# Attention operands laid out by dimension, four heads to a load

## The chip, the cores and the metric

The kernel runs on one core of one Trainium2 chip. The metric is the device time of one execution in microseconds (us), the median of several runs; lower is better.

## The reference

The model is a stack of six residual blocks on x of shape (2, 2048, 256) in float32: an expert layer, attention with 16 heads and a position bias, the expert layer again, a second expert layer, differential attention, and the second expert layer again. The change touches the two attentions. In short:

```python
# first attention, 16 heads of 16
q, k, v = x @ Wq.T + bq, x @ Wk.T + bk, x @ Wv.T + bv
scores = einsum('bhqd,bhkd->bhqk', q, k) / sqrt(16) + slope[h] * (pos_k - pos_q)
y = softmax(causal(scores)) @ v
# second attention, two maps of 16 heads of 16, values of 32
a1, a2 = softmax(causal(q1 @ k1.T * scale)), softmax(causal(q2 @ k2.T * scale))
y = layernorm((a1 - lam[h] * a2) @ v) * (1 - lambda_init) @ Wc
```

## The kernel before

The kernel runs phase after phase. The names in the profile begin with the phase: `ba` is the first attention, `ea` the second, `bp` and `ep` the projections ahead of them, `bo` and `eo` the output products behind them; `ae`, `ce`, `de`, `fe` are the experts.

**Levels.** Queries and keys are float32, but PE multiplies bfloat16. So `project_phase` splits each into three bfloat16 levels (a value is the sum of its levels) and stores them in DRAM, in `lv`, one tensor each for queries and keys, in `ea` for each map: a row of 2048 positions (4 KB) for each level, head and dimension. A score is the sum of six products of levels: the key levels 0, 1, 2 with query level 2 - n, and so on. `KP` = 96 rows of contraction hold them: query level 0 beside key levels 0, 1, 2 (48 rows), query level 1 beside key levels 0, 1 (32 rows), query level 2 beside key level 0 (16 rows), after the order in which the `lq[3 - n]` of the loader names them. On the query side a level is copied n times, on the key side n levels are read. Ahead of these 96 stand `F` rows: in `ba` 12, nine for the position bias and three (`BIAS_MAX`) for the maxima; in `ea` three for the maxima alone.

**Steps.** `attention_phase` works in steps of `HV` = 4 heads (in `ea` two heads of two maps): 8 steps in `ba`, 16 in `ea`. In a step, PE computes all scores twice. The *maxima* products (L1504 into `psA`) have a query to a row; VectorE (DVE) takes the maximum of each row (L1642), splits it in three levels, PE transposes them, and GpSimd's queue (POOL) writes them as three rows into `qx` (`store_maxima`, L1476), where ones in `kx` meet them. The *scores* (L1529 into `psB`) then come out with the maximum subtracted, ScalarE (ACT) exponentiates them (L1624), and PE multiplies them with the values `vx` (L1544). `step_order` writes out the order in which PE, DVE and ACT take the pieces. From slot `NEXT_AT` = 19 of 40 units on, the maxima of the *next* step are mixed in, so PE waits there (L1587) for the next step's `qx` and `kx`; both have two buffers.

**The loader.** SyncE (SP) issues all of this in order, per step (`body`, L1444): the row sums of the step before out to DRAM and back in another shape (`sums_out`); a wait that PE has done with the other buffer; `load` of group 0 (two heads, or the first map) and of `vx`; `inverses_in` (the inverted sums to DRAM, a wait, and four broadcast loads into `rec`); `load` of group 1; and the results to `yT` when POOL has scaled them (L1481). A group has 14 loads: for n = 3, 2, 1 and each of two heads one of queries and one of keys, and two of constants. The core of it:

```python
sp.dma_start(qx[at:at + n * DH, s, hh, :],
             lq[3 - n, rows, :].unsqueeze(0).broadcast_to((n, DH, S)))
sp.dma_start(kx[at:at + n * DH, s, hh, :], lk[0:n, rows, :])
```

Of the kernel before, what the change touches and what calls it, by code (L numbers as in the profile page):

```python
# [1299 lines left out]

def attention_phase(nc, name, D, C, lvq, lvk, vd, yT, sums, sgn, maps, qc, kc, F, MR, s_m, st0):
    two = maps == 2
    steps = B * NHEAD * maps // HV
    KB = F + KP
    shared = qc.shape[0] == F
    VCOL = vd.shape[-1] // KT
    YR = P // maps
    nld = 14
    SR = DH if maps == 1 else VW - 1
    SC = HV * S // P  # L1310
    with Scope(nc, name) as sc:
# [13 lines left out]

        s_ld = [[sc.sem(f"ld{s}{g}") for g in range(2)] for s in range(2)]
        s_v = [sc.sem(f"v{s}") for s in range(2)]
# [64 lines left out]
        with nc.Block() as block:  # L1392

            @block.sync
            def _(sp):
                def load(st, s, *groups):
                    for g in groups:
                        if two:
                            lq, lk, r0, own = lvq[g], lvk[g], st * (2 * DH), slice(g, HV, 2)
                        else:  # L1400
                            lq, lk, r0, own = lvq[0], lvk[0], st * (HV * DH) + g * 2 * DH, slice(2 * g, 2 * g + 2)
                        at = F
                        for n in (3, 2, 1):
                            for h, hh in enumerate(range(HV)[own]):
                                rows = ds(r0 + h * DH, DH)
                                sp.dma_start(qx[at:at + n * DH, s, hh, :],
                                             lq[3 - n, rows, :].unsqueeze(0).broadcast_to((n, DH, S))).then_inc(s_ld[s][g], 16)
                                sp.dma_start(kx[at:at + n * DH, s, hh, :], lk[0:n, rows, :]).then_inc(s_ld[s][g], 16)
                            at += n * DH
                        for dst, src in ((qx, qc), (kx, kc)):  # L1410
                            sp.dma_start(dst[0:F, s, own, :],
                                         src.unsqueeze(1).broadcast_to((F, 2, S)) if shared else
                                         src[ds((st * HV + 2 * g) * F, 2 * F), :].rearrange("(h f) s -> f h s", h=2)
                                         ).then_inc(s_ld[s][g], 16)
                    if 0 in groups:
                        sp.dma_start(vx[:, s].rearrange("p k c -> p (k c)"),
                                     vd[ds(st, 1)].rearrange("g p c -> p (g c)")).then_inc(s_v[s], 16)

# [25 lines left out]
                def body(st, s, use, prev, nxt, before):  # L1444
                    if prev:
                        sums_out(st - 1, 1 - s, use + s - 1)
                    if nxt:
                        if prev:
                            sp.wait_ge(s_av, st * NU)
                        load(st + 1, 1 - s, 0)  # L1450
                    if prev:
                        inverses_in(st - 1, 1 - s, use + s - 1)
                    if nxt:
                        load(st + 1, 1 - s, 1)
                    if prev:
                        for Q in range(QB):
                            result_out(st - 1, 1 - s, Q)

                load(0, 0, 0, 1)

# [36 lines left out]
            def _(pe):  # L1497
                def maxima(i, s, slot):
                    t, k0, m, heads = ITEMS[i]
                    runs = [(hh, b * BLK, k0, m) for b, hh in enumerate(heads)] if len(heads) == 2 else \  # L1500
                        [(heads[0], 0, k0, BLK), (heads[0], BLK, k0 + BLK, m - BLK)]
                    for hh, at, k, n in runs:
                        diag = k + n == (t + 1) * P
                        last = nc.tensor.matmul(psA[:, slot, at:at + n], qx[0:KB, s, hh, t * P:(t + 1) * P],  # L1504
                                                kx[0:KB, s, hh, k:k + n], start=True, stop=not diag)
                        if diag:
                            last = nc.tensor.matmul(psA[:, slot, at + n - P:at + n], C["identb"], C["maskA"],  # L1507
                                                    start=False, stop=True)
                    last.then_inc(s_af, 1)
# [43 lines left out]

                for g in range(2):
                    pe.wait_ge(s_ld[0][g], 16 * nld)
                n = 0
# [15 lines left out]
                def body(st, s, use, prev, nxt, before):  # L1572
# [5 lines left out]
                    for k, a in order:  # L1578
                        if k in RING_KINDS:
                            slot = slots[(k, a)][0]  # L1580
                            pe.wait_ge(*freed[(k, a)])
                        if k == "A":
                            d, i = a
                            if d and not arrived:
                                arrived = True
                                for g in range(2):
                                    pe.wait_ge(s_ld[1 - s][g], 16 * nld * (use + s + 1))  # L1587
                            maxima(i, 1 - s if d else s, slot)
                        elif k == "M":
                            levels(*a, st, s, slot)  # L1590
                        elif k == "C":
                            difference(a, st, s, slot)
                        elif k == "B":
                            scores(*a, st, s, not prev)
                        elif k == "V" and a < 0:
                            values(NU - 1, st - 1, 1 - s)
                        elif k == "V":
                            values(a, st, s)
# [287 lines left out]
def bf16(a):  # L1886
    return np.asarray(a, np.float32).astype(mybir.dt.np(BF16))
# [12 lines left out]

BIAS_ROWS, BIAS_MAX = 12, 3

# [7 lines left out]
def constants():  # L1910
# [28 lines left out]
    for st in range(steps):  # L1939
        for hh in range(HV):  # L1940
            for l, s in enumerate(three_levels(np.float32(SLOPES[st % (NHEAD // HV) * HV + hh]))):
                r = 3 * l if l == 0 else 3 * l + 3
                q[st, hh, r], k[st, hh, r] = -(j // BLK) * BLK, s
                q[st, hh, r + 1], k[st, hh, r + 1] = s, j // P * P
                q[st, hh, r + 2], k[st, hh, r + 2] = s, j % P
            k[st, hh, BIAS_MAX:BIAS_MAX + 3] = 1
    return {
        "c_f32": np.concatenate([f[n] for n, _ in F32_CONSTS], 1).astype(np.float32),
        "c_f16": row(p).astype(np.float16), "c_bf16": bf16(np.concatenate([h[n] for n, _ in BF16_CONSTS], 1)),
        "c_q": bf16(q.reshape(-1, S)), "c_k": bf16(k.reshape(-1, S)),  # L1950
        "c_q1": bf16(np.zeros((3, S))), "c_k1": bf16(np.ones((3, S))),
    }
# [33 lines left out]
def macaron_kernel(nc, D, out):  # L1986
# [6 lines left out]
    routed = scratch("routed", (T + P, H))  # L1993
    lv = [scratch(f"lv{i}", (3, B * H, S), BF16) for i in range(4)]
    vd0, vd1 = scratch("vd0", (B * NHEAD // 4, P, KT * 4 * VW)), scratch("vd1", (B * NHEAD // 2, P, KT * 2 * VW))
    yT, sums = scratch("yT", (B * NHEAD * VW, S)), scratch("sums", (2, 2, HV * S))
    with Scope(nc, "all") as sc:
# [27 lines left out]
        with Scope(nc, "b") as f:  # L2025
            xnT = f.sb("xnT", [P, HC, T])
            norm_phase(nc, "bn", x, xnT, C["ident"])
            project_phase(nc, "bp", D, xnT, [(D["L0_wq"], D["L0_bqk"], DH ** -0.5), (D["L0_wk"], None, 1.0)],
                          D["L0_wv"], D["L0_bv"], lv[0:2], vd0, False)
        attention_phase(nc, "ba", D, C, lv[0:1], lv[1:2], vd0, yT, sums, None, 1, D["c_q"], D["c_k"], BIAS_ROWS, BIAS_MAX, s_m, 0)  # L2030
        output_phase(nc, "bo", D, C, x, yT, D["L0_wo"], 1.0, False)
        experts0("c", 1)
        experts1("d", 0)
        with Scope(nc, "e") as g:
            sgn = g.sb("sgn", [P, B * NHEAD // 2])
            lambda_phase(nc, "el", D, C, sgn[:])
            with Scope(nc, "ef") as f:
                xnT = f.sb("xnT", [P, HC, T])
                norm_phase(nc, "en", x, xnT, C["ident"])
                s = DH ** -0.5  # L2040
                project_phase(nc, "ep", D, xnT, [(D["L1_wq1"], None, s), (D["L1_wk1"], None, 1.0),
                                                 (D["L1_wq2"], None, s), (D["L1_wk2"], None, 1.0)],
                              D["L1_wv"], None, lv, vd1, True)
            attention_phase(nc, "ea", D, C, [lv[0], lv[2]], [lv[1], lv[3]], vd1, yT, sums, sgn, 2, D["c_q1"], D["c_k1"], 3, 0, s_m,
                            B * NHEAD // HV)
# [12 lines left out]
def lay_out(I):  # L2058
# [7 lines left out]
    D["L0_w"] = np.concatenate(up + [I["L0_ffn_w2"].transpose(0, 2, 1)], 2)  # L2066
    for n in "qkv":
        D["L0_w" + n] = by_chunk(I["L0_attn_W" + n].T)
    D["L0_bqk"] = np.concatenate([I["L0_attn_b" + n].reshape(HC, P).T for n in "qk"], 1)
    D["L0_bv"] = I["L0_attn_bv"]  # L2070
# [7 lines left out]
    for k, n in (("rg", "routed_gate_w"), ("ru", "routed_up_w"), ("rd", "routed_down_w")):  # L2078
        D["L1_" + k] = I["L1_ffn_" + n]
    for n in ("q1", "q2", "k1", "k2", "v", "c"):  # L2080
        D["L1_w" + n] = by_chunk(I["L1_attn_W" + n])
# [19 lines left out]
```

## Time and profile before

| | us |
|---|---|
| median of 3 runs | 6779.74 (6776.26 to 6789.61) |
| the profiled execution | 6790.24 |
| its span, first to last instruction | 6788.4 |
| `ba`, first load issued to last score | about 904 to 2022 |
| `ea`, the same | about 3756 to 5944 |
| mean granted clock of PE | 0.877 |

The two attention phases make up nearly half of the span. Rows of the profile name an engine, the line of the kernel, and what is written from what (`ba_kx<-lv`); "<-" behind a wait names what ended it. SPq is SP's queue of transfers, PE the matmul engine. A DMA share is the mean over the core's 16 DMA engines, so 0.13 can mean two of them busy all the time.

### The profile page before, as it was taken

Reading aid. Unit: us, or ns where it says so; the run is one execution under the profiler, and the core shown is the slowest. Engines: PE = TensorE matmul, PEld = TensorE weight load, DVE = VectorE, ACT = ScalarE, POOL = GpSimd, SP = SyncE. Lnnn points to the kernel's source line nnn. Section 1 sums busy time; section 2 is a strip of 40 time slices with the busy share of each in tenths; the row PEclk is TensorE's granted clock in tenths of the full one; section 3 lists DMA queues with packets and bytes.
Section 4 is the critical chain, followed back from the end, with each engine's and each line's share of the span. In section 5 each row is a group of like instructions: output and inputs, shape, how many; then the busy total and the mean of one; then the engine's idle time right before and its main releaser. Section 6 shows DMA issues by size and latency. Waiting matters only on the chain. (4 is left out here: it accounts for less than half of the span.)

```text
span 6788.4 us, 95548 instructions
## 1 busy us (share of the span) xinstructions
PE 5217.8 (77%) x30112; PEld 2794.8 (41%) x30112; DVE 3361.2 (50%) x5679; ACT 2483.8 (37%) x4942; POOL 1576.2 (23%) x1276
## 2 busy tenths in 40 slices
PE   6466448888787466489968688878888888976997
PEld 3355223333235355247953233323333333343696
DVE  7511646666544821311148566756666666533111
ACT  2011106555561011122211266656655655612221
POOL 2388300000101178433324000000000000002332
PEclk9688769999898678789989699989998999988998
DMA  2376431112203177507955211111111111011498
GB/s 93 98 150 138 132 111 41 42 42 59 64 21 116 31 169 149 137 2 243 330 174 163 64 34 35 55 43 35 40 53 41 34 43 53 15 63 35 146 325 272
DMA packets 454298, 660.17 MB, mean 97 GB/s; under 512 B 97984, under 2 KB 308992, under 8 KB 448672
## 3 DMA queue, kind: packets, MB, share of 16 engines
q1 hardware_dynamic: 383232, 544.50, 25.6%
q0 software_dynamic: 70656, 110.44, 8.0%
q8 instruction: 228, 3.74, 0.2%
q14 instruction: 182, 1.49, 0.1%
HBM read 489.33 MB, written 164.20 MB: 96 GB/s over the span
## 5 line engine op out<-in xcount | busy, mean ns | idle before, releaser
L1642 DVE TENSOR_REDUCE ea_mx<-ea_psA 128x1 f32<-128x1024 f32 (+7 forms) x1280 | 1317.6, 1061 | 697.5 <-PE ea_psA L1507 491.4
L1624 ACT ACTIVATE ea_pr<-ea_psB 128x512 f32<-128x512 f32 (+3 forms) x2560 | 1229.7, 535 | 934.6 <-PE ea_psB L1529 514.5
L1504 PE MATMUL ea_psA<-ea_kx,ea_qx 99*128 99x512 bf16 (+3 forms) x2560 | 730.0, 363 | 285.4 <-DMA ea_kx<-in_c_k 256.0
L1642 DVE TENSOR_REDUCE ba_mx<-ba_psA 128x1 f32<-128x1024 f32 (+7 forms) x640 | 657.4, 1061 | 381.5 <-PE ba_psA L1507 282.5
L1529 PE MATMUL ea_psB<-ea_qx,ea_kx 99*128 99x512 bf16 (+3 forms) x2560 | 782.7, 354 | 29.0 <-issue 21.0
L1624 ACT ACTIVATE ba_pr<-ba_psB 128x512 f32<-128x512 f32 (+3 forms) x1280 | 610.7, 535 | 494.8 <-PE ba_psB L1529 260.3
L1544 PE MATMUL ea_psO<-ea_pr,ea_vx 128*32 128x512 f32 (+3 forms) x5120 | 612.2, 551 | 1.9 <-ACT ea_pr L1624 0.4
L1504 PE MATMUL ba_psA<-ba_kx,ba_qx 108*128 108x512 bf16 (+3 forms) x1280 | 371.7, 369 | 198.2 <-DMA ba_kx<-in_c_k 181.3
L1504 PEld LDWEIGHTS ea_psA<-ea_kx,ea_qx 99*128 99x128 bf16 x2560 | 217.9, 100 | 695.1 <-issue 383.4
L1476 POOL DMA_DIRECT2D ea_qx<-ea_mT x192 | 106.0, 559 | 1546.3 <-DVE ea_mT L1664 1521.9
L1529 PEld LDWEIGHTS ea_psB<-ea_qx,ea_kx 99*128 99x128 bf16 x2560 | 242.3, 99 | 501.0 <-ACT ea_pr L1624 315.2
L1529 PE MATMUL ba_psB<-ba_qx,ba_kx 108*128 108x512 bf16 (+3 forms) x1280 | 387.3, 354 | 12.9 <-issue 6.4
L1544 PE MATMUL ba_psO<-ba_pr,ba_vx 128*32 128x512 f32 (+3 forms) x2560 | 305.1, 549 | 1.2 <-ACT ba_pr L1624 0.4
L1504 PEld LDWEIGHTS ba_psA<-ba_kx,ba_qx 108*128 108x128 bf16 x1280 | 109.2, 101 | 409.0 <-issue 231.9
L1476 POOL DMA_DIRECT2D ba_qx<-ba_mT x96 | 53.1, 560 | 804.2 <-DVE ba_mT L1664 804.0
L1507 PE MATMUL ea_psA<-all_cb 128*128 128x128 bf16 x1024 | 229.4, 235 | 0.0
L690 POOL DMA_INDIRECT acc<-ce_y,c_idx x128 | 205.1, 1602 | 46.0 <-issue 35.2
L1529 PEld LDWEIGHTS ba_psB<-ba_qx,ba_kx 108*128 108x128 bf16 x1280 | 120.1, 99 | 231.6 <-ACT ba_pr L1624 154.7
L690 POOL DMA_INDIRECT acc<-ae_y,a_idx x128 | 204.7, 1599 | 46.2 <-issue 36.1
L1532 PE MATMUL ea_psB<-all_cb 128*128 128x128 bf16 x1024 | 209.2, 222 | 0.0
L1481 POOL TENSOR_TENSOR ea_rec<-ea_osb,ea_rec 128x2048 f32<-128x2048 f32 x16 | 72.5, 4532 | 541.1 <-DMA ea_rec<-sums 541.1
L767 DVE TENSOR_TENSOR ae_h<-ae_sg,ae_psH 128x256 f32<-128x256 f32 x64 | 27.0, 422 | 303.0 <-ACT ae_sg L748 269.0
(522 smaller groups left out, 8297.0 us busy)
## 6 DMA issues: line engine op xcount, KB each, us to landing
de_wg<-in_L_rg SPq DMA_DIRECT2D x64, 512.0 KB
de_wu<-in_L_ru SPq DMA_DIRECT2D x64, 512.0 KB
de_wd<-in_L_rd SPq DMA_DIRECT2D x64, 512.0 KB
fe_wg<-in_L_rg SPq DMA_DIRECT2D x64, 512.0 KB
fe_wu<-in_L_ru SPq DMA_DIRECT2D x64, 512.0 KB
fe_wd<-in_L_rd SPq DMA_DIRECT2D x64, 512.0 KB
ae_w<-in_L_w SPq DMA_DIRECT2D x64, 384.0 KB, 3.7
ce_w<-in_L_w SPq DMA_DIRECT2D x64, 384.0 KB
```

The costliest lines, as they stand in the source:

```text
L690: nc.gpsimd.indirect_dma_start(out=acc[a], out_offset=column(n, a), in_=y[:, n % RING, a, :], in_offset=None, bounds_check=bound, oob_is_e ...
L767: nc.vector.tensor_tensor(h[:, u % 2, :], sg[:, u % 2, :], psH[:, u % 2, 1, :], ALU.mult).then_inc(s_hh, 1)
L1476: pool.dma_start(qx[MR:MR + 3, s, hh, t0 * P:(t0 + tc) * P].rearrange("l (t q) -> l t q", q=P), mT[hh * 3 * tc:(hh + 1) * 3 * tc, k, :]).t ...
L1481: nc.gpsimd.tensor_tensor(rec[:, s, :], osb[:, s, :], rec[:, s, :], ALU.mult).then_inc(s_z, 1)
L1504: last = nc.tensor.matmul(psA[:, slot, at:at + n], qx[0:KB, s, hh, t * P:(t + 1) * P], kx[0:KB, s, hh, k:k + n], start=True, stop=not diag)
L1507: last = nc.tensor.matmul(psA[:, slot, at + n - P:at + n], C["identb"], C["maskA"], start=False, stop=True)
L1529: last = nc.tensor.matmul(psB[:, slot, off:BLK], kx[0:KB, s, hh, kt * P:(kt + 1) * P], qx[0:KB, s, hh, Q * BLK + off:(Q + 1) * BLK], start ...
L1532: last = nc.tensor.matmul(psB[:, slot, off:off + P], C["identb"], C["maskB"], start=False, stop=True)
L1544: last = nc.tensor.matmul(psO[hh * VW:(hh + 1) * VW, off:BLK], vx[:, s, kt, vcol:vcol + VW], pr[:, j % 2, hh, off:BLK], start=(kt == 0), s ...
L1624: nc.scalar.activation(pr[:, j % 2, hh, off:BLK], psB[:, exp_slot(n, s), off:BLK], ACT.Exp).then_inc(s_exp, 1)
L1642: v.tensor_reduce(out, src, AX.X, ALU.max).then_inc(s_ar, 1)
```

## The change

The levels are stored in DRAM by dimension, with the four heads of a step side by side, so that the rows of one dimension of four heads are 16 KB in a piece. To that end the columns of the projection weights are reordered on the way in (`together`), and in `ea` the stores of the two maps interleave (`of_map`). `load` is split into `load_queries` (three loads of queries for all four heads, one of the bias rows in `ba`, and `vx`) and `load_keys` (three, and one in `ba`); queries go where group 0 went, keys where group 1 went. The rows of levels now begin at row 0, the nine bias rows follow, and the three rows of the maxima stand last; the ones in `kx` that meet them are loaded once, for both buffers, at the start of a phase. The maxima products leave out these last three rows (`KA`); the scores have them (`KB`). Of the 28 operand loads of a step and that of `vx`, 9 are left in `ba` and 7 in `ea`.

```diff
--- before.py
+++ after.py
@@ -1298,14 +1298,14 @@
-def attention_phase(nc, name, D, C, lvq, lvk, vd, yT, sums, sgn, maps, qc, kc, F, MR, s_m, st0):
+def attention_phase(nc, name, D, C, lvq, lvk, vd, yT, sums, sgn, maps, qc, kc, ones, F, s_m, st0):
     two = maps == 2
     steps = B * NHEAD * maps // HV
-    KB = F + KP
-    shared = qc.shape[0] == F
+    KA, KB = KP + F, KP + F + 3
+    MR = KA
     VCOL = vd.shape[-1] // KT
     YR = P // maps
-    nld = 14
+    nld = 8 if F else 6
     SR = DH if maps == 1 else VW - 1
@@ -1323,7 +1323,7 @@
-        s_ld = [[sc.sem(f"ld{s}{g}") for g in range(2)] for s in range(2)]
+        s_ld, s_one = [sc.sem(f"ld{s}") for s in range(2)], sc.sem("one")
         s_v = [sc.sem(f"v{s}") for s in range(2)]
@@ -1393,28 +1393,27 @@
             def _(sp):
-                def load(st, s, *groups):
-                    for g in groups:
-                        if two:
-                            lq, lk, r0, own = lvq[g], lvk[g], st * (2 * DH), slice(g, HV, 2)
-                        else:
-                            lq, lk, r0, own = lvq[0], lvk[0], st * (HV * DH) + g * 2 * DH, slice(2 * g, 2 * g + 2)
-                        at = F
-                        for n in (3, 2, 1):
-                            for h, hh in enumerate(range(HV)[own]):
-                                rows = ds(r0 + h * DH, DH)
-                                sp.dma_start(qx[at:at + n * DH, s, hh, :],
-                                             lq[3 - n, rows, :].unsqueeze(0).broadcast_to((n, DH, S))).then_inc(s_ld[s][g], 16)
-                                sp.dma_start(kx[at:at + n * DH, s, hh, :], lk[0:n, rows, :]).then_inc(s_ld[s][g], 16)
-                            at += n * DH
-                        for dst, src in ((qx, qc), (kx, kc)):
-                            sp.dma_start(dst[0:F, s, own, :],
-                                         src.unsqueeze(1).broadcast_to((F, 2, S)) if shared else
-                                         src[ds((st * HV + 2 * g) * F, 2 * F), :].rearrange("(h f) s -> f h s", h=2)
-                                         ).then_inc(s_ld[s][g], 16)
-                    if 0 in groups:
-                        sp.dma_start(vx[:, s].rearrange("p k c -> p (k c)"),
-                                     vd[ds(st, 1)].rearrange("g p c -> p (g c)")).then_inc(s_v[s], 16)
+                def load_queries(st, s):
+                    at = 0
+                    for n in (3, 2, 1):
+                        src = lvq[3 - n, ds(st * HV * DH, HV * DH), :].rearrange("(d h) s -> d (h s)", h=HV)
+                        sp.dma_start(qx[at:at + n * DH, s].rearrange("p h s -> p (h s)"),
+                                     src.unsqueeze(0).broadcast_to((n, DH, HV * S))).then_inc(s_ld[s], 16)
+                        at += n * DH
+                    if F:
+                        sp.dma_start(qx[KP:KA, s].rearrange("p h s -> p (h s)"), qc[ds(st * F, F), :]).then_inc(s_ld[s], 16)
+                    sp.dma_start(vx[:, s].rearrange("p k c -> p (k c)"),
+                                 vd[ds(st, 1)].rearrange("g p c -> p (g c)")).then_inc(s_v[s], 16)
+
+                def load_keys(st, s):
+                    at = 0
+                    for n in (3, 2, 1):
+                        sp.dma_start(kx[at:at + n * DH, s].rearrange("p h s -> p (h s)"),
+                                     lvk[0:n, ds(st * HV * DH, HV * DH), :].rearrange("l (d h) s -> l d (h s)", h=HV)
+                                     ).then_inc(s_ld[s], 16)
+                        at += n * DH
+                    if F:
+                        sp.dma_start(kx[KP:KA, s].rearrange("p h s -> p (h s)"), kc[ds(st * F, F), :]).then_inc(s_ld[s], 16)
@@ -1447,16 +1446,19 @@
                             sp.wait_ge(s_av, st * NU)
-                        load(st + 1, 1 - s, 0)
+                        load_queries(st + 1, 1 - s)
                     if prev:
...
                     if nxt:
-                        load(st + 1, 1 - s, 1)
+                        load_keys(st + 1, 1 - s)
                     if prev:
...
-                load(0, 0, 0, 1)
+                load_queries(0, 0)
+                load_keys(0, 0)
+                for u in range(2):
+                    sp.dma_start(kx[KA:KB, u], ones.unsqueeze(1).broadcast_to((3, HV, S))).then_inc(s_one, 16)
@@ -1501,8 +1503,8 @@
                         diag = k + n == (t + 1) * P
-                        last = nc.tensor.matmul(psA[:, slot, at:at + n], qx[0:KB, s, hh, t * P:(t + 1) * P],
-                                                kx[0:KB, s, hh, k:k + n], start=True, stop=not diag)
+                        last = nc.tensor.matmul(psA[:, slot, at:at + n], qx[0:KA, s, hh, t * P:(t + 1) * P],
+                                                kx[0:KA, s, hh, k:k + n], start=True, stop=not diag)
                         if diag:
@@ -1551,8 +1553,8 @@
-                for g in range(2):
-                    pe.wait_ge(s_ld[0][g], 16 * nld)
+                pe.wait_ge(s_ld[0], 16 * nld)
+                pe.wait_ge(s_one, 32)
                 n = 0
@@ -1583,8 +1585,7 @@
                                 arrived = True
-                                for g in range(2):
-                                    pe.wait_ge(s_ld[1 - s][g], 16 * nld * (use + s + 1))
+                                pe.wait_ge(s_ld[1 - s], 16 * nld * (use + s + 1))
                             maxima(i, 1 - s if d else s, slot)
@@ -1898,7 +1899,7 @@
-BIAS_ROWS, BIAS_MAX = 12, 3
+BIAS_ROWS = 9
@@ -1939,16 +1940,15 @@
             for l, s in enumerate(three_levels(np.float32(SLOPES[st % (NHEAD // HV) * HV + hh]))):
-                r = 3 * l if l == 0 else 3 * l + 3
+                r = 3 * l
                 q[st, hh, r], k[st, hh, r] = -(j // BLK) * BLK, s
...
                 q[st, hh, r + 2], k[st, hh, r + 2] = s, j % P
-            k[st, hh, BIAS_MAX:BIAS_MAX + 3] = 1
     return {
...
         "c_f16": row(p).astype(np.float16), "c_bf16": bf16(np.concatenate([h[n] for n, _ in BF16_CONSTS], 1)),
-        "c_q": bf16(q.reshape(-1, S)), "c_k": bf16(k.reshape(-1, S)),
-        "c_q1": bf16(np.zeros((3, S))), "c_k1": bf16(np.ones((3, S))),
+        "c_q": bf16(q.transpose(0, 2, 1, 3).reshape(-1, HV * S)),
+        "c_k": bf16(k.transpose(0, 2, 1, 3).reshape(-1, HV * S)), "c_one": bf16(np.ones((3, S))),
     }
@@ -1991,7 +1991,7 @@
     routed = scratch("routed", (T + P, H))
-    lv = [scratch(f"lv{i}", (3, B * H, S), BF16) for i in range(4)]
+    lvq, lvk = (scratch(n, (3, B * NHEAD * 2 * DH, S), BF16) for n in ("lvq", "lvk"))
     vd0, vd1 = scratch("vd0", (B * NHEAD // 4, P, KT * 4 * VW)), scratch("vd1", (B * NHEAD // 2, P, KT * 2 * VW))
@@ -2026,8 +2026,8 @@
             project_phase(nc, "bp", D, xnT, [(D["L0_wq"], D["L0_bqk"], DH ** -0.5), (D["L0_wk"], None, 1.0)],
-                          D["L0_wv"], D["L0_bv"], lv[0:2], vd0, False)
-        attention_phase(nc, "ba", D, C, lv[0:1], lv[1:2], vd0, yT, sums, None, 1, D["c_q"], D["c_k"], BIAS_ROWS, BIAS_MAX, s_m, 0)
+                          D["L0_wv"], D["L0_bv"], [lvq[:, 0:B * H], lvk[:, 0:B * H]], vd0, False)
+        attention_phase(nc, "ba", D, C, lvq, lvk, vd0, yT, sums, None, 1, D["c_q"], D["c_k"], D["c_one"], BIAS_ROWS, s_m, 0)
         output_phase(nc, "bo", D, C, x, yT, D["L0_wo"], 1.0, False)
@@ -2038,10 +2038,11 @@
                 s = DH ** -0.5
+                of_map = lambda a, g: a.rearrange("l (r g) s -> l g r s", g=2)[:, g]
                 project_phase(nc, "ep", D, xnT, [(D["L1_wq1"], None, s), (D["L1_wk1"], None, 1.0),
                                                  (D["L1_wq2"], None, s), (D["L1_wk2"], None, 1.0)],
-                              D["L1_wv"], None, lv, vd1, True)
-            attention_phase(nc, "ea", D, C, [lv[0], lv[2]], [lv[1], lv[3]], vd1, yT, sums, sgn, 2, D["c_q1"], D["c_k1"], 3, 0, s_m,
+                              D["L1_wv"], None, [of_map(a, g) for g in range(2) for a in (lvq, lvk)], vd1, True)
+            attention_phase(nc, "ea", D, C, lvq, lvk, vd1, yT, sums, sgn, 2, None, None, D["c_one"], 0, s_m,
                             B * NHEAD // HV)
@@ -2064,9 +2065,11 @@
     D["L0_w"] = np.concatenate(up + [I["L0_ffn_w2"].transpose(0, 2, 1)], 2)
-    for n in "qkv":
-        D["L0_w" + n] = by_chunk(I["L0_attn_W" + n].T)
-    D["L0_bqk"] = np.concatenate([I["L0_attn_b" + n].reshape(HC, P).T for n in "qk"], 1)
+    together = lambda a, heads: a.reshape(-1, NHEAD // heads, heads, DH).transpose(0, 1, 3, 2).reshape(-1, H)
+    for n in "qk":
+        D["L0_w" + n] = by_chunk(together(I["L0_attn_W" + n].T, HV))
+    D["L0_wv"] = by_chunk(I["L0_attn_Wv"].T)
+    D["L0_bqk"] = np.concatenate([together(I["L0_attn_b" + n], HV).reshape(HC, P).T for n in "qk"], 1)
     D["L0_bv"] = I["L0_attn_bv"]
@@ -2077,7 +2080,9 @@
         D["L1_" + k] = I["L1_ffn_" + n]
-    for n in ("q1", "q2", "k1", "k2", "v", "c"):
+    for n in ("q1", "q2", "k1", "k2"):
+        D["L1_w" + n] = by_chunk(together(I["L1_attn_W" + n], HV // 2))
+    for n in ("v", "c"):
         D["L1_w" + n] = by_chunk(I["L1_attn_W" + n])
```

## Rows read from the trace of the kernel before

**Rows 1.** the page, its first line and part 1 (busy us, share, xinstructions)
```profile
span 6788.4 us, 95548 instructions
...
PE 5217.8 (77%) x30112; PEld 2794.8 (41%) x30112; DVE 3361.2 (50%) x5679; ACT 2483.8 (37%) x4942; POOL 1576.2 (23%) x1276
```

**Rows 2.** waits of PE (total us, times, longest): `ba`, `ea`, and the whole span
```profile
PE ba_psA L1504 <- DMA ba_kx<-in_c_k: 122.5, 6, 21.6
...
PE ea_psA L1504 <- DMA ea_kx<-in_c_k: 202.3, 14, 15.3
PE ea_psA L1504 <- DVE ea_mx L1642: 24.9, 43, 0.7
...
PE ea_psA L1504 <- DMA ea_kx<-in_c_k: 256.0, 15, 53.6
...
PE ba_psA L1504 <- DMA ba_kx<-in_c_k: 181.3, 7, 58.8
```

**Rows 3.** timeline of PE at one step's stall (start, length, what, [idle before])
```profile
1189.28 0.26 PE L1504 MATMUL ba_psA<-ba_kx,ba_qx 108*128 108x128 bf16 x1 [19.98 <-DMA ba_kx<-in_c_k]
```

**Rows 4.** timeline of SP's queue, one `ba` step (start us, length us)
```profile
1125.28 0.83 SPq L1406 DMA_DIRECT2D ba_qx<-lv  x1
...
1138.50 0.36 SPq L1416 DMA_DIRECT2D ba_vx<-vd  x1
1138.93 0.41 SPq L1428 DMA_DIRECT2D sums<-ba_sm  x1
1157.51 1.73 SPq L1433 DMA_DIRECT2D ba_rec<-sums  x4
1159.43 0.78 SPq L1406 DMA_DIRECT2D ba_qx<-lv  x1
...
1166.95 2.60 SPq L1408 DMA_DIRECT2D ba_kx<-lv  x1
...
1174.15 0.32 SPq L1411 DMA_DIRECT2D ba_kx<-in_c_k  x1
1175.01 0.44 SPq L1442 DMA_DIRECT2D yT<-ba_rec  x1
```

**Rows 5.** windows; the last three numbers are PE clock, DMA share, GB/s
```profile
1137.00:1145.50 8.50, 8.50 (x60) 3.20 (x59) 6.95 (x7) 6.09 (x12) 0.00 (x0) 1.00 0.87 176
...
1158.90:1163.70 4.80, 4.80 (x30) 1.48 (x30) 3.59 (x4) 3.81 (x8) 0.00 (x0) 1.00 0.90 200
1163.70:1167.00 3.30, 3.30 (x21) 1.20 (x20) 2.70 (x3) 2.41 (x6) 2.45 (x1) 1.00 0.18 58
1167.00:1172.50 5.50, 2.30 (x15) 0.47 (x12) 2.89 (x7) 2.54 (x5) 2.09 (x1) 1.00 0.19 75
...
1182.00:1186.00 4.00, 0.00 (x0) 0.00 (x0) 0.00 (x0) 0.00 (x0) 0.00 (x0) 0.50 0.13 51
...
3981.00:3984.50 3.50, 3.50 (x25) 0.94 (x25) 2.71 (x4) 2.98 (x7) 0.00 (x0) 1.00 0.21 81
```

**Rows 6.** DMA issues: count, KB each, median us to landing
```profile
ea_qx<-lv SPq DMA_DIRECT2D x64, 192.0 KB
...
ba_vx<-vd SPq DMA_DIRECT2D x8, 1024.0 KB, 18.9
ba_rec<-sums SPq DMA_DIRECT2D x32, 256.0 KB, 4.5
...
ba_qx<-in_c_q SPq DMA_DIRECT2D x16, 96.0 KB
...
ea_qx<-in_c_q SPq DMA_DIRECT2D x32, 24.0 KB
```

**Rows 7.** PE by form: busy us, mean ns, for both contraction lengths of L1504
```profile
L1504 PE MATMUL ba_psA<-ba_kx,ba_qx 108*128 108x512 bf16 x896 | 300.6, 399 | 15.1 <-DVE ba_mx L1642 13.3
...
L1504 PE MATMUL ea_psA<-ea_kx,ea_qx 99*128 99x512 bf16 x1792 | 590.0, 392 | 27.6 <-DVE ea_mx L1642 24.4
```

**Rows 8.** the page, part 3: DMA queue, packets, MB, share of 16 engines
```profile
q8 instruction: 228, 3.74, 0.2%
```

## The prediction

> **What bounds the kernel now.** I read the page first: TensorE (PE) has the largest share, 77%, but this is a mean over many stages [rows 1]. Next I asked what PE waits for in the two attention phases. There one wait stands out: the first maxima product of a step (L1504, behind the waits for `s_ld`) waits for the operand loads of the next step. It is 122.5 us in six steps of the first phase (`ba`) and 202.3 us in fourteen of the second (`ea`). The next wait of PE there is 24.9 us in all of `ea`, and the longest single waits, 58.8 and 53.6 us, are the first loads of each phase [rows 2]. In the timeline one such wait is 19.98 us of nothing, ended by the last load [rows 3]. So in these twenty steps the loads set the period, one for one; time taken off them is gained until the wait is gone.
>
> Then I followed SP's queue through one `ba` step [rows 4]. Loads of the first two heads go out from 1125.28, `vx` at 1138.50, and the write of the inverses at 1138.93; SP then waits for that write until 1157.51, issues `rec`, the loads of the other two heads from 1159.43 to 1174.5, then yT. PE goes on at 1189.28. The chain is 1189.28 − 1125.28 = 64.0 us. Is it issue or transfer? The windows tell [rows 5]: from 1182 to 1186 the DMA share is 0.13 and 51 GB/s move. 0.13 × 16 = 2.1, so two engines work and fourteen are idle, at 51 / 2 = 25.5 GB/s each. From 1167 to 1172.5 it is 0.19 × 16 = 3.0 engines. These are the loads of two and three copies. SP issues a load in under 0.8 us, but some stretch, to 2.6 us here [rows 4], where it waits for room: the engines are behind, not SP.
>
> I add up the fullest engine, in KB of 1024 bytes, with the sizes of [rows 6]. A load of three copies, 192 KB over three engines, gives it 64; of two copies, 128 KB over two, 64; of one, 64 KB over 16, 4. Half a step's loads (four of each) are 528, the constants 16 (two loads of 8 per engine), `vx` 64, `rec` (four loads of 256 KB) 64. So the first half has 528 + 16 + 64 = 608 KB or 24.4 us at 25.5 GB/s, the second with `rec` 608 KB or 24.4 us. That is 49 of the 64 us. The other 15 us are the start of each half and the stretches in which all sixteen engines move `vx`, `rec`, yT and the loads of one copy: 176 to 200 GB/s at a share of 0.87 to 0.90, or 13 to 14 GB/s for each engine, half of 25.5 [rows 5].
>
> **The change, part by part.** *Fewer loads.* Queries go as three loads (three, two, one copies) of four heads, keys likewise, so 28 operand loads become 8 or 6. The leading dimension of each is still the number of copies, so I expect three, two and sixteen engines again. Per engine the three-copy load carries 768 / 3 = 256 KB, the two-copy 512 / 2 = 256, the one-copy 16: 528 KB, as now. `ba`'s constants are 9 rows of 16 KB, 16 KB on each of nine engines, as now. So for `ba`: **no byte less on the fullest engine**, and the work that SP saves (some 10 issues of 0.7 to 0.8 us in each half) is hidden behind it: SP would only wait sooner, at the inverses and at the end. If that cover were gone, the issues would cost about 14 us a step. The rule "Use all 16 engines" in the Trainium skill (DMA: Bandwidth & Descriptors, Rules for kernel authors) says this of such loads: a leading dimension of c copies confines a transfer to at most c engines; the trace agrees, with 0.13 and 0.19 of sixteen. That rule speaks against a large gain here, as the rows do.
>
> *No constants in `ea`.* 16 KB less on the fullest engine in each half: 32 KB, 32.8 / 25.5 = 1.3 us a step, 14 × 1.3 = 18 us.
>
> *Longer rows.* One row is now 16 KB, not 4. No row of the loads prices this. One end is no gain. The other is the best rate of a three-engine stretch, 81 / 3 = 27 GB/s [rows 5]: 557 kB in 20.6 us, not 21.8, so 1.2 us a half. Most stretches lie at 25.5, so I take 0.5 us, 1.0 a step: 6 us in `ba`, 14 us in `ea`. A far row is the instruction queue: 228 packets of 16.4 KB took 0.2% (0.15 to 0.25) of sixteen engines' span, 0.7 to 1.2 us each, or 14 to 23 GB/s [rows 8]. Another destination, so I leave it out of the sum; at 17 GB/s each half would grow by 11 us, 440 us in all.
>
> *Order.* Queries and `vx` stay ahead of the inverses, keys behind `rec`, where the halves were. SP now reaches the inverses earlier, but the write waits behind the same queries on the same engines. yT may go out about 5 us sooner and then runs beside the three-copy keys in place of the two-copy ones: the same loss, moved.
>
> *First loads.* PE's first wait now has `vx` ahead of the keys and two loads of ones behind them: 64 + 32 KB more in `ba`, 98 kB, 3.9 us, less 1 us for rows; in `ea` 32 + 32 − 32 (no constants) = 32 KB, 1.3 us, less 1. Together +3 us.
>
> *Rows of maxima.* They move behind the others; the maxima product now reads 105 or 96 rows, not 108 or 99. A product of 512 columns takes 399 ns with 108 rows and 392 with 99 [rows 7]: nothing. POOL's stores keep number and size. They may stand behind one 16 KB packet, 0.6 us at 25.5 GB/s; PE asks for them units of work later. Uncovered, it would be 0.5 us three times a step. The stores of the projection keep runs of 1 KB, every second row in `ea`: nothing.
>
> **Sum**: −6 − 14 − 18 + 3 = −35 us. The profiled execution, 6790 us with its 6788.4 us span, would become 6755. It stands 10.5 us above the median shown, 6779.74, so against that I say **6745 us**, 0.5% faster. In `ba` the wait of 20.4 us stays above 18, in `ea` 14.5 becomes 12.
>
> **The rivals.** *A, the number of loads sets the time.* If each load carried a cost of its own, 20 fewer would undo the stall: 6780 − 325 [rows 2] = 6455 us. Against it: the two engines that are never idle. The Trainium skill (same page and section) advises coalescing many small transfers, since under 64 KB mostly overhead is paid; by that advice the one-copy loads at least would be cheaper, but no run here shows it. Chance 0.05.
>
> *B, nothing that can be measured*, which for this kernel is anything within 0.2% (14 us). Long rows bring nothing, and the 18 us of the constants are eaten by `vx` in the first wait or by a collision that moves: 6766 to 6793, about 6772. Chance 0.17.
>
> *C, slower: the slow start of a broadcast lasts as long as the broadcast.* From 1163.7 to 1167, the first 3.3 us of three-copy loads, the engines move 58 GB/s at a share of 0.18; later, at 0.19, it is 75 [rows 5]. Three engines begin on copies of the same rows in step, and something they share holds them up; after one load of 64 KB each they are out of step. Now the first broadcast is four times as long. At 58 GB/s, 786 kB take 13.6 us, at 78 10.1: 3.5 us, of which 0.8 are paid today, so +2.7 us a step, 20 × 2.7 = 54. With the −35 it is +19: **6799 us**. From 1.8 us a step upwards it turns the sign; if the keys, which aren't broadcast, suffered too, 6853. For it: the slow starts recur. Against it: it may be the start of a queue, not the copying. Chance 0.16, the 16 KB packet of [rows 8] included.
>
> **How the numbers follow.** The forecast (gains of 14 to 90 us) has 0.62, A 0.05, B 0.17, C 0.16. Faster by over 0.2%: 0.62 + 0.05 = 0.67; within: 0.17; slower: 0.16. The low end: 6745 less 32 us if the slow starts vanish (0.8 × 2 × 20) and less 28 for the rest of the row bound (0.7 × 2 × 20), rounded: 6685. The high end takes in B and C's 6799 with the rows bringing nothing (+10 to 20): 6815. Outside lie A, the dear end of C and the slow packet.
>
> **What would show it.** Right: PE's waits on the loads near 116 us in `ba` and 170 in `ea`; again stretches at 0.13 and 51 GB/s, before the inverses land and before PE goes on; SP's queue with four or five short issues and no stretched ones; a gap from the first query load to `rec` still near 31 us. A is right if the gaps are gone; C if the stretch near 58 GB/s grows from 3 to 10 us or more. The forecast is wrong if the two-engine stretches are absent, or if the engine rate with 16 KB rows isn't 25 to 27 GB/s.

## The result, and the profile after

The changed kernel takes **7007.6 us** (median of 4 runs, 7006.5 to 7012.4) against 6782.7 for the one before: a ratio of 1.0333, 95% interval 1.0315 to 1.0351. It is 225 us slower, where 35 us less was forecast.

The page of the changed kernel, first line and part 1. The span has grown by 216 us. PE is busy only 25 us longer than in [rows 1], with the same products at a mean granted clock of 0.868 for 0.877, so nearly all of the time went into waiting.

```profile
span 7004.6 us, 94559 instructions
...
PE 5242.8 (75%) x30108; PEld 2791.8 (40%) x30112; DVE 3370.2 (48%) x5679; ACT 2483.8 (35%) x4942; POOL 1570.4 (22%) x1276
```

Waits of PE in the changed kernel, in `ba` and then in `ea` (total us, times, longest):

```profile
PE ba_psA L1506 <- DMA ba_kx<-in_c_k: 177.0, 6, 31.0
PE ba_psA L1506 <- DMA ba_kx<-in_c_one: 69.3, 1, 69.3
...
PE ea_psA L1506 <- DMA ea_kx<-lvk: 249.0, 14, 19.4
PE ea_psA L1553 <- POOL ea_rec L1483: 93.4, 15, 18.5
PE ea_psA L1506 <- DMA ea_kx<-in_c_one: 63.3, 1, 63.3
```

Against [rows 2] the loads cost 54.5 us more in `ba` and 46.7 in `ea`, and the two first waits 20.2 more. In `ea` PE also waits for POOL's product with the inverses (L1553). 18.5 us of it stand at the end of the phase, as they did before; the other 74.9 us, in fourteen steps, are new. POOL's product needs `rec`, which now lands later, so I read this as the same lateness seen earlier in the step. Together these are 196 of the 216 us.

SP's queue in one `ba` step of the changed kernel (start us, length us):

```profile
1135.53 2.37 SPq L1400 DMA_DIRECT2D ba_qx<-lvq  x3
1138.12 0.28 SPq L1404 DMA_DIRECT2D ba_qx<-in_c_q  x1
1138.59 0.36 SPq L1405 DMA_DIRECT2D ba_vx<-vd  x1
1146.78 0.35 SPq L1427 DMA_DIRECT2D sums<-ba_sm  x1
1172.87 1.72 SPq L1432 DMA_DIRECT2D ba_rec<-sums  x4
1174.69 2.00 SPq L1411 DMA_DIRECT2D ba_kx<-lvk  x3
1176.78 0.34 SPq L1416 DMA_DIRECT2D ba_kx<-in_c_k  x1
```

The issues are few and short, as the change says: the queries and `vx` are out in 3.4 us, the keys in 2.4. But from the first query load to `rec` it is 37.3 us, not 32.2 [rows 4], and from `rec` until PE goes on at 1210.54 it is 37.7, not 31.8: each half has grown by 5 to 6 us. The windows of this step show where (the last two numbers are DMA share and GB/s):

```profile
1149.00:1158.50 9.50, 9.50 (x75) 4.08 (x71) 6.69 (x8) 5.90 (x14) 0.00 (x0) 1.00 0.19 57
...
1190.50:1199.00 8.50, 0.00 (x0) 0.00 (x0) 0.00 (x0) 0.00 (x0) 0.00 (x0) 0.50 0.18 54
```

A share of 0.18 to 0.19 is three busy engines, as from 1167 to 1172.5 before [rows 5]. But they move 54 to 57 GB/s and not 75, for some 9 us in each half, with the queries (copies) and with the keys (three levels) alike.

### The profile page after: what moved, and what is told of

The parts are those of the page before. It is cut to its first block and busy times, and to the rows that moved or that the text cites. A ratio compares the mean times of both kernels' runs of the same rounds, so it can differ in the third digit from the quotient of the medians.

```text
span 7004.6 us, 94559 instructions
## 1 busy us (share of the span) xinstructions
PE 5242.8 (75%) x30108; PEld 2791.8 (40%) x30112; DVE 3370.2 (48%) x5679; ACT 2483.8 (35%) x4942; POOL 1570.4 (22%) x1276
## 5 line engine op out<-in xcount | busy, mean ns | idle before, releaser
L1506 PE MATMUL ea_psA<-ea_kx,ea_qx 96*128 96x512 bf16 (+3 forms) x2560 | 734.9, 364 | 341.5 <-DMA ea_kx<-lvk 249.0
L1506 PE MATMUL ba_psA<-ba_kx,ba_qx 105*128 105x512 bf16 (+3 forms) x1280 | 370.1, 367 | 264.1 <-DMA ba_kx<-in_c_k 177.0
L1506 PEld LDWEIGHTS ea_psA<-ea_kx,ea_qx 96*128 96x128 bf16 x2560 | 218.8, 100 | 753.1 <-issue 309.1
L1506 PEld LDWEIGHTS ba_psA<-ba_kx,ba_qx 105*128 105x128 bf16 x1280 | 109.0, 101 | 473.6 <-issue 206.5
L1546 PEld LDWEIGHTS ea_psO<-ea_pr,ea_vx 128*32 128x32 f32 x5120 | 102.0, 109 | 176.8 <-ACT ea_pr L1625 88.5
```

The source lines that it names most:

```text
L1506: last = nc.tensor.matmul(psA[:, slot, at:at + n], qx[0:KA, s, hh, t * P:(t + 1) * P], kx[0:KA, s, hh, k:k + n], start=True, stop=not diag)
L1546: last = nc.tensor.matmul(psO[hh * VW:(hh + 1) * VW, off:BLK], vx[:, s, kt, vcol:vcol + VW], pr[:, j % 2, hh, off:BLK], start=(kt == 0), s ...
```

## The experiments

Two theories stood first. *P, place*: engines that write SBUF partitions 32 apart at the same time share a way in and halve each other. With three copies as the leading dimension, engine 0 should have rows 0 to 15 and engine 2 rows 32 to 47, and both go through them in step. (No row here names the engine of a row; this division is assumed, and the loads below fit it.) *S, source*: they read the same rows, or levels at a fixed distance, in step. A third, *O*, was the order: all queries, `vx` and one-copy loads early.

### The loads alone

This kernel leaves the model out and makes test loads, one after the other, each waited for but the last four. It ran once, so each time in the table is a single measurement. In `far` the groups come from far-apart rows, in `copies` they are the same rows; the second number is the first partition written.

```python
far = lambda l, n, w=HV * S: src.rearrange("(l r) s -> l r s", l=l)[:, 0:n, 0:w]
copies = lambda l, n, w=HV * S: src[0:n, 0:w].unsqueeze(0).broadcast_to((l, n, w))
tests = (("two4", 0, far(2, 4)), ("two8", 0, far(2, 8)), ("two16", 0, far(2, 16)), ("two32", 0, far(2, 32)),
         ("two32at32", 32, far(2, 32)), ("two32copies", 0, copies(2, 32)), ("three16", 0, far(3, 16)),
         ("three16at32", 32, far(3, 16)), ("wide48", 0, far(3, 16).rearrange("l r s -> r l s")))
```

> This kernel leaves the whole model out: it loads x and the constants, makes eleven test loads one after another, each waited for, and writes x out. The loads carry rows of 16 KB with two or three groups of rows as the leading dimension, so that two or three engines share the work. A row alone took 0.61 us in the changed kernel, so two16 (16 rows per engine) is about 9.8 us plus some 2.5 us of latency. Theory P (the place in SBUF: engines that write partitions 32 apart at the same time halve each other): two4, two8 and two16 undisturbed, 5, 7.5 and 12.5 us; two32 (partitions 0 to 31 and 32 to 63) doubled, about 42 us and not 22; two32copies the same 42; three16 about 20 and not 12.5; two32at32 and three16at32 show whether the halves 0 to 63 and 64 to 127 are separate (22 and 12.5) or not (42 and 20). Theory S (the source in DRAM: copies of one row, or levels at a fixed distance, are read in step): two32copies and two32 differ, and three16at32 is like three16. Short rows: short16 (4 KB rows) 5 us, a few tenths more with a collision; fourshort about 12.5 us. wide48 (dimension first, 16 engines) 4 to 6.5 us.

In SP's queue the next start is the end of a test. The trace drops the digits that end a name: `m_two` at 32.29 is two16, at 44.81 two32, and `m_three` is three16. `m_short` and `m_fourshort` are three groups of 16 rows of 4 KB at partition 0, one load and four.

```profile
32.29 13.06 SPq L2023 DMA_DIRECT2D m_two<-in_c_q  x2
...
44.81 0.54 SPq L2023 DMA_DIRECT2D m_two<-in_c_q  x1
79.13 0.64 SPq L2023 DMA_DIRECT2D m_two32at<-in_c_q  x1
101.36 0.53 SPq L2023 DMA_DIRECT2D m_two32copies<-in_c_q  x1
138.69 0.76 SPq L2023 DMA_DIRECT2D m_three<-in_c_q  x1
157.44 0.72 SPq L2023 DMA_DIRECT2D m_three16at<-in_c_q  x1
169.90 0.63 SPq L2023 DMA_DIRECT2D m_wide<-in_c_q  x1
177.58 0.73 SPq L2025 DMA_DIRECT2D m_short<-in_c_q  x1
183.88 2.94 SPq L2028 DMA_DIRECT2D m_fourshort<-in_c_q  x4
197.91 0.40 SPq L1982 DMA_DIRECT2D out_x<-all_x  x1
```

| load, two or three groups of 16 KB rows | partitions | us |
|---|---|---|
| two16, 16 apart | 0 to 31 | 12.5 |
| two32, 32 apart | 0 to 63 | 34.3 |
| two32copies, the same source rows | 0 to 63 | 37.3 |
| two32at32, 32 apart across 64 | 32 to 95 | 22.2 |
| three16 | 0 to 47 | 18.8 |
| three16at32 | 32 to 79 | 12.5 |
| wide48, 16 engines, 48 rows | 0 to 47 | 7.7 |
| short16, three groups of 4 KB rows | 0 to 47 | 6.3 |
| fourshort, four of these | 0 to 47 | 14.0 |

Windows of two32, two32at32, three16, three16at32 and wide48 (the last two numbers are DMA share and GB/s):

```profile
46.00:78.00 32.00, 0.00 (x0) 1.00 0.12 33
81.00:100.00 19.00, 0.00 (x0) 1.00 0.12 52
...
140.00:156.00 16.00, 0.00 (x0) 1.00 0.16 48
159.50:169.00 9.50, 0.00 (x0) 1.00 0.18 78
171.50:176.00 4.50, 0.00 (x0) 1.00 0.86 135
```

Two engines move 52 GB/s when partition 64 lies between them and 33 when it doesn't, with the same bytes from the same rows. So the place decides. Theory S falls with it: three16 and three16at32 read the same rows and differ by a third. (Copies were 3 us slower than far rows, 37.3 for 34.3; that is left open.) P holds with the halves 0 to 63 and 64 to 127 apart. It was 34.3 us and not the doubled 42 that was expected; that the engines are in step for only part of the time would explain it, but isn't shown. A three-copy load at the change's place costs 18.8 − 12.5 = 6.3 us too much. The Trainium skill (SBUF — State Buffer, Door 1: The DMA port swizzle) has this map: four neighbours share a port, 32 further on is the same port, 64 further on another. These loads agree, 33 against 52 GB/s.

### The same loads at other partitions

```diff
-                    at = 0
                     for n in (3, 2, 1):
+                        at = {3: 32, 2: 0, 1: 80}[n]
```

The same in both loaders; the line `at += n * DH` goes.

> The changed kernel with the same loads in the same order, but the 48 rows of the three-copy load at partitions 32 to 79, the two-copy load at 0 to 31. Theory P with separate halves: engine 0 writes 32 to 47 and engine 2 64 to 79, no collision, so the loads run at 0.61 us a row and the time is near 6750 to 6830 us. Theory P without separate halves, theory S (source) and theory O (order: queries, one-copy loads and vx all early) leave it at 7007 within 15 us.

6754.1 us, ratio to the kernel before 0.9963 (0.995 to 0.9977). Only row numbers differ, and it takes 253 us less than the changed kernel. SP's queue in a `ba` step, and PE's waits, in `ba` and in `ea`:

```profile
1132.17 2.54 SPq L1400 DMA_DIRECT2D ba_qx<-lvq  x3
...
1163.82 1.84 SPq L1430 DMA_DIRECT2D ba_rec<-sums  x4
```

```profile
PE ba_psA L1504 <- DMA ba_kx<-in_c_k: 110.1, 6, 19.4
PE ba_psA L1504 <- DMA ba_kx<-in_c_one: 69.1, 1, 69.1
...
PE ea_psA L1504 <- DMA ea_kx<-lvk: 161.6, 14, 12.1
PE ea_psA L1504 <- DMA ea_kx<-in_c_one: 58.0, 1, 58.0
```

From the first query load to `rec` it is 31.7 us, where the changed kernel took 37.3: 5.7 us less for one three-copy load, near the 6.3 of the load alone. Three engines move 82 and 79 GB/s from 1144 to 1155. The new part of the wait for POOL is gone as well. The first waits hardly fell, by 0.2 and 5.3 us, so nearly all of the 253 us comes from the 20 steps with two three-copy loads each, about 6 us a load.

### The same place, another time

```diff
-                    at = 0
-                    for n in (3, 2, 1):
+                    for n in (2, 3, 1):
+                        at = {3: 0, 2: 48, 1: 80}[n]
```

Again in both loaders.

> The changed kernel, same partitions and same rows of 16 KB, but the two-copy load issued ahead of the three-copy load. Engine 2 then has the three-copy load to itself while engines 0 and 1 carry the two-copy load, so that engines 0 and 2 don't write 32 partitions apart at the same time. Theory P (the collision needs both, place and time): back to what e3_other_partitions gave, 6740 to 6780 us. If the partitions or the row length are slow whatever runs beside them: 7007.

6748.4 us, ratio 0.9944 (0.9927 to 0.996). Partitions and rows are those of the changed kernel; by the order of the loads, engines 0 and 2 no longer write their shares of the three-copy load at the same time. The first half is 31.4 us long (1133.20 to 1164.59), and three engines move 82 and 79 GB/s again. So it takes both, place and time.

### Shorter rows

For each head, and for each two heads, a load of its own, in the layout and order of the changed kernel (queries shown, for each head; keys likewise; `nld` becomes 26 or 24, and 14 or 12 with two heads):

```diff
-                        sp.dma_start(qx[at:at + n * DH, s].rearrange("p h s -> p (h s)"),
-                                     src.unsqueeze(0).broadcast_to((n, DH, HV * S))).then_inc(s_ld[s], 16)
+                        for h in range(HV):
+                            sp.dma_start(qx[at:at + n * DH, s, h, :],
+                                         src[:, h * S:(h + 1) * S].unsqueeze(0).broadcast_to((n, DH, S))).then_inc(s_ld[s], 16)
```

> The changed kernel with its DRAM layout and its order (all queries, constants, vx, then all keys), but a load for each head again: rows of 4 KB, 26 or 24 operand loads a step. Theory P: engines in step on partitions 32 apart get out of step after the first short load, so the time goes back to the one before or a little below: 6740 to 6800 us. Theory O: the order costs the time, and it stays at 6980 to 7010.

> The changed kernel with two heads to a load, rows of 8 KB. Theory P with getting out of step after the first load of a stretch: half the bytes of the three-copy part run in step, so about half of the loss between short rows (6790) and long rows (7007): 6880 to 6920 us. If the length of the row alone decides (8 KB in step all the time): 6990 to 7010; if only 16 KB rows are slow: 6790.

6789.8 us with rows of 4 KB (1.0018, 1.0005 to 1.0032), 6903.3 with 8 KB (1.0167, 1.0138 to 1.0196), and 7007.6 with 16 KB (1.0333). Theory O falls: order and layout together cost about 12 us (3 to 22 by the interval). Against the undisturbed 0.9963 the losses are 0.0055, 0.0204 and 0.037, or 0.15, 0.55 and 1 of the whole. One load of a stretch in step and the following ones out of step would give 0.25, 0.5 and 1. That is near, and the loads alone point the same way: one short load took 6.3 us, and four took 14.0, only 1.5 more than the same bytes undisturbed. With 8 KB rows a three-engine stretch begins at 58 GB/s (1145 to 1149) and goes on at 66 and 70. No trace shows the step of single engines, so this part is argued.

### The kernel before at other partitions

```diff
-                        at = F
                         for n in (3, 2, 1):
+                            at = F + {3: 32, 2: 0, 1: 80}[n]
```

> The kernel before with the three-copy load 32 partitions further on (44 to 91 in ba, 35 to 82 in ea) and the two-copy load in its place, so that engines 0 and 2 never write 32 partitions apart in one half. Theory P: the slow start of each three-copy stretch (58 GB/s for 3 us, then 75) goes, 0.8 to 1.5 us a half step, 1.6 to 3 us in 20 steps: 6720 to 6750 us. Otherwise the same as before, 6781.

6768.2 us, 0.9976 (0.9965 to 0.9987). The slow start in [rows 5] was the same collision: where it was 58 GB/s, the three-engine stretch now begins at 78 (1163 to 1166). It costs the kernel before about 16 us, half of the least that was expected (31).

### Dimension first

The changed kernel and the kernel before, with the dimension as the leading one and the copies or levels second. Queries and keys are turned alike, so the rows of contraction still match. The edit is shown in the changed kernel; the kernel before gets the same two edits in its own loads.

```diff
-                                     src.unsqueeze(0).broadcast_to((n, DH, HV * S))).then_inc(s_ld[s], 16)
+                                     src.unsqueeze(1).broadcast_to((DH, n, HV * S))).then_inc(s_ld[s], 16)
-                                     lvk[0:n, ds(st * HV * DH, HV * DH), :].rearrange("l (d h) s -> l d (h s)", h=HV)
+                                     lvk[0:n, ds(st * HV * DH, HV * DH), :].rearrange("l (d h) s -> d l (h s)", h=HV)
```

> The changed kernel with the dimension as the leading one of each operand load and the copies or levels second, on both sides, so that the rows of contraction keep matching. If the loads of two and three engines set the time, as both traces say, sixteen engines take them: 96 KB per engine for half a step in place of 528. The waits for the operand loads (177 and 249 us in the changed kernel, 122 and 202 in the one before) should vanish, and the first loads shrink from 63 to 69 us to about 20: 6400 to 6480 us. If instead something else behind the loads (the inverses' trip through DRAM, POOL's product) takes over as the wait, 6500 to 6600. If the number of engines doesn't matter, 7000.

> The kernel before, with its 28 operand loads a step, its rows of 4 KB and its order, and only the dimension made the leading one of each load (sixteen engines). If what the fullest engine carries set the time, the waits for the loads go as in e1_dimension_first (6391 us). What is left of a difference to that run is the price of 20 more issues a step (0.7 to 0.8 us each on SP) once nothing hides them: chain of loads 64 us before, now about 30 us of issue and the inverses' trip, under the 44 us at which PE begins to wait, so 6390 to 6430 us. If issues do matter (theory of the change's own words), PE waits again: 6450 to 6600.

**6391.6 us** (0.9428, 0.9409 to 0.9447) and **6373.8 us** (0.9391, 0.9374 to 0.9408): both beat both kernels, and both lie below the ranges expected. The changed kernel with this edit, SP's queue in a `ba` step and the window of its first half:

```profile
1104.35 2.06 SPq L1400 DMA_DIRECT2D ba_qx<-lvq  x3
...
1123.08 1.73 SPq L1432 DMA_DIRECT2D ba_rec<-sums  x4
```

```profile
1104.30:1123.00 18.70, 18.34 (x134) 7.05 (x135) 14.74 (x17) 13.18 (x30) 2.17 (x4) 1.00 0.85 153
```

The first half takes 18.7 us and not 37.3. The share is 0.85 at 153 GB/s, with `vx` in it: 153 / (0.85 × 16) = 11 for each engine, less than half of 25.5, but sixteen work and not three. PE no longer waits for loads within a step; the first waits are 38.5 and 32.0 us. The kernel before with the edit still issues 28 operand loads:

```profile
1095.63 0.66 SPq L1406 DMA_DIRECT2D ba_qx<-lv  x1
...
1113.80 1.73 SPq L1433 DMA_DIRECT2D ba_rec<-sums  x4
```

18.2 us, so twenty issues more a step cost nothing even without the cover of slow loads. The gain can be added up for this run: the waits within steps (324.8 us) are gone, the first waits have fallen from 58.8 and 53.6 to 31.7 and 29.1 (51.6), and PE is busy 35.2 us less with the same products, at a mean granted clock of 0.902 for 0.877. That is 411.6 of the 413.7 us by which the span is shorter. Of the 18 us between the two kernels I suspected the first loads:

```diff
+                for u in range(2):
+                    sp.dma_start(kx[KA:KB, u], ones.unsqueeze(1).broadcast_to((3, HV, S))).then_inc(s_one, 16)
                 load_queries(0, 0)
                 load_keys(0, 0)
-                for u in range(2):
-                    sp.dma_start(kx[KA:KB, u], ones.unsqueeze(1).broadcast_to((3, HV, S))).then_inc(s_one, 16)
+                load_values(0, 0)
```

`vx` gets a function of its own, `load_values`, for this; within the steps its place stays.

> e1_dimension_first with another order of the very first loads of a phase: the two loads of ones ahead, then queries, keys, and vx last, as the kernel before has it. PE's first waits were 38.5 and 32.0 us in e1_dimension_first, 31.7 and 29.1 in e2_dimension_first_before. If vx ahead of the keys and the ones behind them (1 MB and two loads on three engines) are the difference, the first waits fall to about 31 and 29, some 10 us less in all: 6380 us. If the layout or the order within a step costs the rest, it stays at 6391.

> The same kernel as e2_dimension_first_before, again beside e8_first_loads on one chip. 6374 us if the two hardly differ: then neither 20 loads fewer nor rows of 16 KB bring anything once all engines carry the loads.

6386.1 us (0.9412, 0.9397 to 0.9427) and 6379.1 (0.9405, 0.939 to 0.942): the intervals overlap, so what is left between the two layouts can't be told from nothing, and neither can what the order of the first loads brings to the time. The traces do show it: PE's first waits are 34.1 and 28.2 us with the new order, for 38.5 and 32.0, 8.2 less together, where 10 were expected.

## Why the prediction was wrong

- *The loads set the period*: right. With the loads out of the way, 390 to 410 us go, more than the 325 of rival A, since the first waits fall too and PE's work gets shorter.
- *Two and three engines carry them, the fullest has the same bytes, issues are hidden*: right. Rival A, that the number of loads sets the time, is refuted twice: fewer loads didn't help, and with sixteen engines 28 loads are as good as 8. The 14 us a step that the issues were to cost without their cover didn't appear either (18.2 us for 18.7).
- ***Longer rows*: this is the step that failed.** I took 0.5 us less for each half, −20 us in all, with no gain as the other end of this term; a loss stood in rival C alone. Measured, each half grew by 5.1 and 5.9 us in the step above, and the kernel by 225. Undisturbed, the term was fair: with the collision taken out by place or by time the kernel runs at 0.9963 and 0.9944, 25 and 38 us below the one before, around the −35 of the sum; PE's waits are then 110 us in `ba` and 162 to 166 in `ea`, near the 116 and 170 forecast. (The kernel before has a collision of its own, worth 16 us, that is gone in these two runs. So not all of the 25 and 38 us are the forecast's terms, and that they come so near to 35 is partly luck.) What failed is the assumption that three engines keep their rate when the rows are longer. Two of them write partitions 32 apart and get in each other's way for longer than with short rows. The far row, a packet at 14 to 23 GB/s, had no part in it: two undisturbed engines moved 52 GB/s with the same 16 KB rows.
- *Rival C* had the effect (the slow start grows with the length, here from 3.3 to over 9 us, the sign it named) and the wrong cause and price. It is not the copying: keys are hit as much. It was priced at 2.7 us a load with the mean of three engines, 58 for 78 GB/s, of which by theory P one isn't disturbed; a load cost about 6 us, and PE waits for the slowest of the three. Even its dear end, 6853, was 155 us short.
- *First loads*: +3 forecast, 20 measured; 15 are left with the loads at other partitions (69.1 and 58.0 us for 58.8 and 53.6). With sixteen engines the order of the first loads was worth 8.2 us of PE's waits; what it is worth with two or three wasn't measured.
- *Constants in `ea`*: with 4 KB rows the waits in `ea` fell by 202.3 − 192.6 = 9.7 us, for 18 forecast; order and layout differ as well there, so the term by itself wasn't measured. *Rows of maxima*: nothing, as said: 397 ns for a product of 512 columns with 105 rows, for 399 in [rows 7].

## What to carry to other kernels

Before merging loads, count what the fullest DMA engine carries: a leading dimension of 2 or 3 leaves the work to 2 or 3 engines, however few or many the loads are. Put the dimension that 16 divides first, here worth 6% with one line on each side; the rows of contraction must be reordered alike for queries and keys. And where few engines write at once, look at which partitions they write at the same time; with long rows a collision lasts longer.

## What the runs showed of the hardware

- Two engines writing 32 partitions apart in one half of SBUF moved 33 GB/s, and across partition 64 they moved 52. 16 apart they took 12.5 us for 256 KB each, as fast as three engines that don't meet.
- Three engines on partitions 0 to 47 took 18.8 us for 48 rows of 16 KB, and 12.5 on partitions 32 to 79. The cost grows with the row: with 4, 8 and 16 KB rows the kernel took 1.0018, 1.0167 and 1.0333 of the time before. That the engines stay in step through a long row and fall out of step after a short load fits this, but isn't shown.
- Sixteen engines writing 48 neighbouring partitions (wide48) moved 135 GB/s at a share of 0.86, or 135 / (0.86 × 16) = 9.8 each, far less than the 26 of one of two alone, and still 1.7 times as much as three (78).
